# A decoder layer with fast-weight memory and routed experts: a new order of the router stage and other loads around it

## The chip, the cores and the metric

The kernel runs on one NeuronCore of one Trainium2 chip. The metric is the device time of one execution in microseconds (us). TensorE, VectorE (DVE), ScalarE (ACT), GpSimd (POOL) and SyncE (SP) each run their own instruction list in order and meet at semaphores; DMA transfers are issued by SyncE, ScalarE or GpSimd.

## What is computed

The layer takes x of 4 x 1024 x 512 and a context of 4 x 64 x 512, all in float32. It has three parts, each added onto x. Layer norm, softmax and top-k are the usual ones:

```python
x = x + attn(layernorm(x), W_qkv, W_out)          # 16 heads of 64, rotary, causal softmax
x = x + xattn(layernorm(x), ctx, ctx, Wq, Wk, Wv, Wo, bo, ...)
x = x + ffn(layernorm(x), router_w, router_b, we_gate, we_up, we_down)

# xattn: a memory M (32 x 32 per batch and head) is built from the 64 context rows
#   M = M - a * (M k) k^T + b * v k^T      row by row, k normalised
#   q = layernorm_per_head(query @ Wq.T) * gq + bq
#   out = (M q) @ Wo.T + bo
# ffn: top 2 of 8 experts per token, weights by softmax of the two logits
#   y = (silu(h @ we_gate[e]) * (h @ we_up[e])) @ we_down[e]
```

## The kernel before

Every matrix product that needs float32 accuracy is made of three products of a high and a low part (`parts`: high x high, high x low, low x high); the low part is the input less its high part. ScalarE writes high parts, VectorE or GpSimd low ones.

The program has four stages, each a room of buffers and semaphores with a barrier of all engines at its end. `context_phase` prepares context keys and values. `attention_phase` (512 units of one head and one row tile) does attention, and on GpSimd the recurrence of the memory; it leaves the unnormalised head outputs in `scr_attT` and the reciprocals of the softmax sums in `scr_rinv`. `memory_phase`, called the router stage here, goes over 32 tiles of 128 tokens: output projection of attention, residual, memory read-out, second residual, router logits, top 2, a position for each token in its experts' regions, and a scatter of the normalised rows into `scr_hs`. `expert_phase` runs 39 blocks of 256 rows, one expert each.

The router stage is a software pipeline written by hand. `sweep` runs `step(r, i)` on every engine: four steps unrolled, a loop of three rounds of eight steps, eight steps unrolled; so the loop has two back edges. At step i the tiles i, i-1, ... i-4 are at different points. TensorE does, in order: transposes of n2 of tile i-1 (`turn("n")`), the first half of the output projection of tile i into pA, transposes of qn (i-2), the second half, transposes of hn (i-3), the counting product pW (i-4), the query projection pQ (i-1), the memory product pM (i-2), the logits pR (i-3). A turn waits until the turn two before it has been read, so that the turn of hn waits for the low part of nT (`nlo`). At a batch change (i = 2, and then every eighth step) the memory of the next batch, laid out block-diagonally in `bd`, is multiplied by the output weights `wo` in four products of 512 columns into two banks in turn; VectorE must have taken the low part (`mwl`) of a bank's product before the bank is used again, and all four before pM.

VectorE's step in the kernel before: low parts of nT (L1614), qT (L1620) and of the attention rows ap (L1595); x2 = pA + x (L1629), its layer norm (L1601 to L1607), the low parts of a batch change (L1637); the per-head norm of the query (L1644 to L1658); x3 (L1665), its layer norm into hn, and the token column (L1673); logits and top 2 of tile i-3 (L1679 to L1694); positions of tile i-4 (L1702 to L1713). GpSimd adds the bias (x2b, L1398), makes qn = qc * hs3 (L1404), scales the attention rows of tile i+2 (L1389) and scatters tile i-4 (L1414).

Ahead of the first step the router stage loads 3 MB of weights into buffers that are free then, and splits them (L1297, L1522, L1587), behind which TensorE waits. After the last step, VectorE turns the expert counts into a table of blocks (L1721 to L1747), SyncE writes blocks of zeros behind each expert's rows (L1355), and after the barrier `expert_phase` fetches rows and the first weights.

## Time and profile before

| | us |
|---|---|
| median of 3 runs | 3069.8 |
| lowest, highest | 3062.35, 3074.35 |
| profiled execution | 3063.33 (span 3061.6) |
| context and attention, until TensorE stops | 0 to 1692.96 |
| router stage, TensorE's first to last product | 1728.41 to 2276.91 |
| expert stage, from its first product | 2318.96 to 3061.6 |

TensorE is busy for 2732.9 us (89% of the span), VectorE for 1981.9 (65%), ScalarE for 1666.9 (54%), GpSimd for 1481.4 (48%). These shares are means over stages with different limits; the rows further down look at one stage or one step each. In a row of the timeline the first number is the start, the second the duration, and brackets hold the idle time of the engine just before, with what ended it.

### The profile page before, as it was taken

To read this page: it belongs to the slowest core of one execution; us is meant where nothing else is said; L and a number is where in the kernel's file an instruction comes from. 1 tells how busy PE (TensorE), PEld (TensorE's weight loads), DVE (VectorE), ACT (ScalarE), POOL (GpSimd) and SP (SyncE) were. 2 spreads that over 40 slices of the span, in tenths; PEclk is the share of its full clock that TensorE was granted. 3 is DMA by queue.
4 is the path that set the end of the run, shared out by engine and by line. 5 is a ranking of instruction groups with operands and counts; after the bars stand their busy time and mean duration, and the time that the engine had idled before them with its cause. 6 is when DMAs were issued, how large, how long until landed. Compare 5 with 4: busy or idle time off the path is not lost. (4 is left out here: it accounts for less than half of the span.)

```text
span 3061.6 us, 49728 instructions
## 1 busy us (share of the span) xinstructions
PE 2732.9 (89%) x15887; PEld 2288.0 (75%) x15887; DVE 1981.9 (65%) x3907; ACT 1666.9 (54%) x3190; POOL 1481.4 (48%) x1606
## 2 busy tenths in 40 slices
PE   5899979999889999899998498889857999999998
PEld 3788868888778888688887377767645888888886
DVE  5477656677657676566667377778754666565555
ACT  2466655666656665566666233323315767776665
POOL 1567654766555666455564234434423334444443
PEclk8999999999999999999999699999978999999999
DMA  3644343435343434343433545455424444444433
GB/s 120 111 107 116 94 117 91 107 95 131 87 104 95 125 95 113 92 107 84 106 74 80 149 116 127 127 126 136 110 89 116 96 97 103 99 99 97 96 55 48
DMA packets 221099, 316.81 MB, mean 103 GB/s; under 512 B 60432, under 2 KB 139312, under 8 KB 217584
## 3 DMA queue, kind: packets, MB, share of 16 engines
q1 hardware_dynamic: 178256, 220.20, 29.6%
q0 software_dynamic: 42656, 94.31, 12.6%
q8 instruction: 94, 1.54, 0.2%
q14 instruction: 93, 0.76, 0.1%
HBM read 241.28 MB, written 75.17 MB: 103 GB/s over the span
## 5 line engine op out<-in xcount | busy, mean ns | idle before, releaser
L1010 ACT ACTIVATE a_pt<-a_PT 128x512 fp32r<-128x512 f32 (+3 forms) x768 | 350.4, 490 | 534.4 <-PE a_PT L876 533.6
L1084 DVE TENSOR_REDUCE a_nmax<-a_S 128x1 f32<-128x1024 f32 (+7 forms) x512 | 384.9, 752 | 266.7 <-PE a_S L865 265.5
L1093 DVE TENSOR_TENSOR a_pt<-a_PT,a_pt 128x512 fp32r<-128x512 f32 (+3 forms) x768 | 401.8, 550 | 190.6 <-ACT a_pt L1010 188.9
L893 PE MATMUL a_O<-a_pt,a_v 128*128 128x256 f32 (+1 forms) x2560 | 355.9, 286 | 49.5 <-DVE a_ot L1108 25.2
L999 ACT ACTIVATE a_pb<-a_S,a_nmax 128x1024 f32<-128x1024 f32 (+7 forms) x512 | 380.3, 743 | 17.8 <-DVE a_nmax L1084 17.8
L893 PEld LDWEIGHTS a_O<-a_pt,a_v 128*128 128x128 f32 x2560 | 325.9, 193 | 64.7 <-DVE a_ot L1108 30.8
L876 PE MATMUL a_PT<-a_ident,a_pb 128*128 128x128 f32 x2304 | 342.3, 276 | 35.3 <-DVE a_pt L1093 33.9
L1982 DVE TENSOR_TENSOR e_w<-e_raw,e_w 128x1024 fp32r<-128x1024 f32 x238 | 281.2, 1223 | 119.0 <-ACT e_w L1932 118.9
L876 PEld LDWEIGHTS a_PT<-a_ident,a_pb 128*128 128x128 f32 x2304 | 270.5, 141 | 78.5 <-issue 28.5
L863 PE MATMUL a_S<-a_kh,a_qs 128*128 128x512 f32 (+3 forms) x768 | 285.3, 372 | 1.7 <-DMA a_kl<-a_rot 1.7
L813 PE MATMUL a_Z<-early_xT,early_wq 128*128 128x512 f32 x512 | 239.2, 467 | 45.8 <-issue 16.9
L864 PE MATMUL a_S<-a_kl,a_qs 128*128 128x512 f32 (+3 forms) x768 | 258.4, 348 | 0.0
L739 POOL TENSOR_TENSOR a_rot<-a_tmp,a_rot 128x512 fp32r<-128x512 f32 x128 | 163.1, 1294 | 177.6 <-ACT a_rot L982 177.3
L1818 POOL DMA_INDIRECT out<-e_y,e_dest x78 | 140.3, 1798 | 201.4 <-ACT e_y L1941 187.8
L732 POOL TENSOR_TENSOR a_tmp<-a_tmp,a_part 128x512 f32<-128x512 f32 x64 | 82.4, 1287 | 311.8 <-DVE a_part L1059 311.8
L1932 ACT ACTIVATE e_w<-e_raw 128x2048 fp32r<-128x2048 f32 x119 | 227.8, 1914 | 6.6 <-DMA e_raw<-in_we,e_ix 6.2
L1814 POOL DMA_INDIRECT e_raw<-in_we,e_ix x122 | 153.1, 1255 | 153.4 <-issue 135.3
L815 PE MATMUL a_Z<-early_xT,early_wq 128*128 128x512 f32 x512 | 203.7, 398 | 0.0
L814 PE MATMUL a_Z<-early_xT,early_wq 128*128 128x512 f32 x512 | 203.1, 397 | 0.0
L813 PE MATMUL a_Z<-early_wv,early_xT 128*128 128x256 f32 x512 | 162.8, 318 | 2.0 <-DVE a_v L1076 2.0
L863 PEld LDWEIGHTS a_S<-a_kh,a_qs 128*128 128x128 f32 x768 | 147.1, 192 | 21.2 <-DMA a_kl<-a_rot 3.6
L864 PEld LDWEIGHTS a_S<-a_kl,a_qs 128*128 128x128 f32 x768 | 147.3, 192 | 17.3
(286 smaller groups left out, 7005.1 us busy)
## 6 DMA issues: line engine op xcount, KB each, us to landing
a_qs<-a_rot SPq DMA_DIRECT2D x256, 128.0 KB, 2.3
a_kh<-a_rot SPq DMA_DIRECT2D x256, 128.0 KB, 2.3
a_kl<-a_rot SPq DMA_DIRECT2D x256, 128.0 KB, 2.3
e_rows<-scr_hs SPq DMA_DIRECT2D x40, 516.0 KB
scr_attT<-a_ot SPq DMA_DIRECT2D x256, 64.0 KB, 2.1
m_att<-scr_attT SPq DMA_DIRECT2D x32, 512.0 KB, 4.4
m_rb<-scr_rinv SPq DMA_DIRECT2D x64, 256.0 KB, 9.0
a_raw<-in_wqk POOLq DMA_DIRECT2D x31, 512.0 KB, 4.2
```

What stands on the lines that cost most here:

```text
L813: pe.matmul(out, lhs(0), rhs(0), start=start, stop=False)
L815: return pe.matmul(out, lhs(1), rhs(0), start=False, stop=stop)
L863: pe.matmul(out, q, kh[:, sl, c0:c1], start=True, stop=False)
L864: pe.matmul(out, q, kl[:, sl, c0:c1], start=False, stop=c1 != cols)
L876: mm = pe.transpose(PT[(k + s) % 2][:, (kt % 4) * P:(kt % 4 + 1) * P], pb[u % 2][:, kt * P:(kt + 1) * P], ident[:, :])
L893: mm = pe.matmul(O[:, c0:2 * P], v2[:, n % 2, kt, h, :, :].rearrange("p a d -> p (a d)"), pt[j % 2][:, part, kt, c0:2 * P], start=kt == 0 ...
L999: act.activation(pb[u % 2][:, 0:cols], S[u % 2][:, 0:cols], ACT.Exp, bias=nmax[:, u % GU:u % GU + 1], scale=1.0, accum_out=rsum[:, b % 2, ...
L1010: act.activation(pt[u % 2][:, 0, 4 * s:4 * s + m, (qt % 2) * P:(qt % 2 + 1) * P], PT[(k + s) % 2][:, 0:m * P].rearrange("p (k q) -> p k q" ...
L1084: dve.tensor_reduce(nmax[:, u % GU:u % GU + 1], S[u % 2][:, 0:cols], AXX, ALU.max, negate=True).then_inc(s_nb, 1)
L1093: dve.tensor_tensor(pt[u % 2][:, 1, 4 * s:4 * s + m, q], PT[(k + s) % 2][:, 0:m * P].rearrange("p (k q) -> p k q", k=m), pt[u % 2][:, 0, 4 ...
L1932: act.activation(w[:, k, 0, :], raw[:, k, :], ACT.Copy).then_inc(s[f"whi{k}"], 1)
L1982: dve.tensor_tensor(w[:, k, 1, c], raw[:, k, c], w[:, k, 0, c].bitcast(F32), ALU.subtract).then_inc(s[f"wlo{k}"], 1)
```

## The change

**Seam ahead of the router stage.** The buffers `raw`, `cos`, `sin` and `tmp` of attention become parts of one buffer `stage`, which lives through all stages. In unit U-16 GpSimd loads the router stage's weights into it (`load_next`); the router stage splits them into the buffers that attention used for x and its weights. The loads of tile 0 stand ahead of the constants. `rinv` is stored so that a tile's rows are contiguous: one store for a batch, not four, and rows of 4 KB for the broadcast loads.

**Router stage.** The query weights are centred once per head (`centre`), so that the per-head mean of pQ is zero; the reduction, the mean and qc go. ScalarE squares pQ itself. qn is made by VectorE from pQ. The token, top and gap columns of hn go to GpSimd, hn has four slots instead of eight. VectorE's step has a new order, with the layer norm in two parts (`moments`, `norm`). A batch change's four products, high and low parts are spread over the step.

**Seam behind.** The fill positions are computed first; the table of blocks takes fewer, wider instructions. Four of the stores of zeros are issued by ScalarE, and that of the spare block stands ahead of the wait. The three weight matrices of expert 0 are loaded during the router stage, and the first fetch is skipped if the first block belongs to expert 0.

The core of the diff:

```diff
@@ attention_phase
+            def load_next():
+                last = NG * GH // 2 - 1
+                gp.wait_ge(s_zfree, zi[("q", last, 3)] + 1)
+                gp.wait_ge(s_rot, 4 * (last + 1))
+                gp.wait_ge(s_wlow, len(wcount))
+                for k in range(6):
+                    gp.dma_start(stage[:, k // 2, k % 2 * T:(k % 2 + 1) * T],
+                                 io["wmem"][k // 3][:, k % 3 * T:(k % 3 + 1) * T]).then_inc(s_wm, 16)
@@ memory_phase, sync
+            load_att(0, 0)
+            load_x(0, 0)
+            for dst, src in ((bo[:, :], io["bo"].partition_broadcast(P)),
+                             (wo[:, :, :], io["woT"].rearrange("(e p) n -> p e n", p=P))):
+                sp.dma_start(dst, src).then_inc(s["c"], 16)
+            load_att(0, 1)
+            load_x(0, 1)
...
+            sp.dma_start(dram["hs"][NE * REG:NE * REG + BLK, :].rearrange("(a p) d -> p a d", p=P),
+                         zero[:, :, :]).then_inc(s["zero"], 16)
             sp.wait_ge(s["fin"], 1)
-            for e in range(NE):
+            for e in range(NE // 2):
@@ memory_phase, gpsimd
-                    gp.tensor_tensor(qn[:, j % 2, :].rearrange("p (h j) -> p h j", h=XH),
...
+                    gp.tensor_scalar(hn[:, j % 4, C_TOK:C_TOK + 1], hn[:, j % 4, C_TOK:C_TOK + 1],
+                                     float(4 * P), None, ALU.add).then_inc(s["side"], 1)
+                    gp.tensor_tensor(hn[:, j % 4, C_GAP:C_GAP + 1], top8[:, j % QT, 0:1],
+                                     top8[:, j % QT, 1:2], ALU.subtract).then_inc(s["side"], 1)
+                    gp.tensor_copy(hn[:, j % 4, C_TOP:C_TOP + 1], idx[:, j % 2, 0:1]).then_inc(s["side"], 1)
...
+            gp.wait_ge(s["c"], 16 * 6)
+            gp.wait_ge(s["wl"], 6)
+            for k in range(3):
+                gp.dma_start(route["raw"][:, k, :], io["we"][0, k]).then_inc(s["pre"], 16)
@@ memory_phase, scalar
+                    act.wait_ge(s["Q"], t)
+                    act.activation(sq[:, :], pQ[:, :], ACT.Square).then_inc(s["sq"], 1)
...
+            for e in range(NE // 2, NE):
+                z = act.value_load(route["tab"][0:1, 3, e:e + 1], min_val=0, max_val=(NE - 1) * REG + TOK)
+                act.dma_start(dram["hs"][bass.ds(z, BLK), :].rearrange("(a p) d -> p a d", p=P),
+                              zero[:, :, :]).then_inc(s["zero"], 16)
@@ memory_phase, vector
+            def centre(k):
+                w = loaded(k).rearrange("p (h j) -> p h j", j=XD)
+                n = 3 * (k - 4)
+                mean = wmean[:, k - 4, :]
+                dve.tensor_reduce(mean, w, AXX, ALU.add).then_inc(s["wc"], 1)
+                dve.wait_ge(s["wc"], n + 1)
+                dve.tensor_scalar(mean, mean, 1.0 / XD, None, ALU.mult).then_inc(s["wc"], 1)
+                dve.wait_ge(s["wc"], n + 2)
+                dve.tensor_tensor(w, w, mean.unsqueeze(2).broadcast_to([P, 2 * XH, XD]),
+                                  ALU.subtract).then_inc(s["wc"], 1)
...
-                    dve.tensor_reduce(hs1[:, j % 2, :], q3, AXX, ALU.add).then_inc(s["hvar"], 1)
...
-                    dve.tensor_tensor(qc[:, j % 2, :].rearrange("p (h j) -> p h j", h=XH), q3,
...
+                    dve.tensor_tensor(qn[:, j % 2, :].rearrange("p (h j) -> p h j", h=XH),
+                                      pQ[:, :].rearrange("p (h j) -> p h j", h=XH),
+                                      hs3[:, j % 2, :].unsqueeze(2).broadcast_to([P, XH, XD]),
+                                      ALU.mult).then_inc(s["qn"], 1)
...
             ch.step(dve.tensor_copy(cnt[:, :], pW[:, 0:NE]))
+            ch.step(dve.tensor_tensor(fill[:, :], cnt[:, :], base[:, :], ALU.add))
+            dve.tensor_copy(route["tab"][:, 3, 0:NE], fill[:, :]).then_inc(s["fin"], 1)
@@ expert_phase, vector
-            ch.do(dve.memset(same[:, 0:1], 0.0))
+            ch.do(dve.tensor_scalar(same[:, 0:1], route["expert"][:, 0:1], 0.0, None, ALU.is_equal))
```

VectorE in a plain step of the router stage, from the add into x2 on. m_A0 is pA of tile i, m_Q the query projection, m_W the counts. Before:

```order
L1629 TENSOR_TENSOR m_x2<-m_A0,m_x 128x512
L1601 BN_STATS m_st<-m_x2 128x6
...
L1607 TENSOR_SCALAR m_n2<-m_x2,m_mv,m_rs 128x512
L1644 TENSOR_REDUCE m_hs1<-m_Q 128x16
L1645 ISA
L1648 TENSOR_SCALAR m_hs3<-m_hs1 128x16
L1651 TENSOR_TENSOR m_qc<-m_Q,m_hs3 128x512
L1655 TENSOR_REDUCE m_hs1<-m_sq 128x16
L1658 RECIPROCAL m_hs3<-m_hs2 128x16
L1665 TENSOR_TENSOR m_x3<-m_M,m_x2b 128x512
```

and now:

```order
L1718 TENSOR_TENSOR m_x2<-m_A0,m_x 128x512
L1677 BN_STATS m_st<-m_x2 128x6
...
L1679 BN_AGGR m_mv<-m_st 128x2
L1728 TENSOR_TENSOR m_pr<-m_W,m_base 128x8
L1729 TENSOR_TENSOR m_cum<-m_cum,m_msum 128x8
L1734 SCALAR_TENSOR_TENSOR m_junk,m_pf<-m_iota8,m_idx,m_pr 128x8 x2
L1739 CAST m_pi<-m_pf 128x2
L1684 RECIPROCAL m_rs<-m_sd 128x1
L1686 TENSOR_SCALAR m_n2<-m_x2,m_mv,m_rs 128x512
L1747 TENSOR_REDUCE m_hs1<-m_sq 128x16
L1755 TENSOR_TENSOR m_x3<-m_M,m_x2b 128x512
```

The counting of tile i-4 has moved from the end of the step to between the moments and the normalisation of x2, and three instructions on m_Q are gone from between n2 and the reduction of the squares.

TensorE at a batch change, where the products of bd and wo stand. Before:

```order
L1439 MATMUL m_A0<-m_ww,m_ap 128x512
L1470 ISA
L1477 MATMUL m_A1<-m_wo,m_bd 128x512
L1477 MATMUL m_M<-m_wo,m_bd 128x512
L1476 ISA
L1477 MATMUL m_A1<-m_wo,m_bd 128x512
L1476 REGISTER_ALU
L1477 MATMUL m_M<-m_wo,m_bd 128x512
L1448 MATMUL m_T0<-m_ident,m_hn 128x128 x4
```

and now, with the rows of the projections left out:

```order
L1501 MATMUL m_A1<-m_wo,m_bd 128x512
...
L1472 MATMUL m_A0<-early_xT,m_ap 128x512
L1501 MATMUL m_M<-m_wo,m_bd 128x512
L1481 MATMUL m_T1<-m_ident,m_qn 128x128 x4
...
L1501 MATMUL m_A1<-m_wo,m_bd 128x512
...
L1501 MATMUL m_M<-m_wo,m_bd 128x512
```

The four products stood behind the second half of the projection; now one stands behind the transposes of n2, one between the halves, one behind the second half and one behind the counting product.

## Rows read from the trace of the kernel before

**Rows 1.** Stretches: length, busy time (instructions) by engine, TensorE's clock, DMA share, GB/s.

```profile
1728.41:2276.91 548.50, 472.09 (x2273) 378.73 (x2273) 398.88 (x1136) 165.96 (x304) 216.23 (x156) 0.93 0.46 117
2276.91:2318.96 42.05, 2.18 (x8) 1.44 (x9) 14.77 (x58) 4.22 (x4) 6.69 (x10) 0.50 0.61 226
2318.96:3061.60 742.64, 728.46 (x3432) 589.84 (x3432) 440.71 (x665) 505.31 (x547) 301.27 (x237) 0.99 0.41 85
```

**Rows 2.** TensorE's waits in the router stage: total us, times, longest.

```profile
PE m_T L1448 <- DVE m_nT L1614: 42.0, 26, 4.8
...
PE m_A L1477 <- DVE m_mw L1637: 17.2, 4, 4.8
```

**Rows 3.** Timeline, TensorE, the turn of hn in a plain step.

```profile
2001.24 0.63 PE L1448 MATMUL m_T<-m_ident,m_hn 128*128 128x128 f32 x4 [1.48 <-DVE m_nT L1614]
```

**Rows 4.** Timeline, VectorE, one plain step, some of its rows.

```profile
1990.57 0.68 DVE L1644 TENSOR_REDUCE m_hs<-m_Q 128x16 f32<-128x512 f32 x1
...
1992.88 0.69 DVE L1655 TENSOR_REDUCE m_hs<-m_sq 128x16 f32<-128x512 f32 x1 [0.70 <-ACT m_sq L1567]
1993.95 0.25 DVE L1658 RECIPROCAL m_hs<-m_hs 128x16 f32<-128x16 f32 x1 [0.38 <-ACT m_hs L1569]
...
1996.17 0.16 DVE L1605 RECIPROCAL m_rs<-m_sd 128x1 f32<-128x1 f32 x1 [0.36 <-ACT m_sd L1573]
1996.37 1.68 DVE L1607 TENSOR_SCALAR m_hn<-m_x,m_mv,m_rs 128x512 f32<-128x512 f32 x1
...
1999.55 0.16 DVE L1702 TENSOR_TENSOR m_pr<-m_W,m_base 128x8 f32<-128x8 f32 x1
...
2000.41 0.69 DVE L1614 TENSOR_TENSOR m_nT<-m_T,m_nT 128x512 fp32r<-128x512 f32 x1
...
2005.06 0.55 DVE L1607 TENSOR_SCALAR m_n<-m_x,m_mv,m_rs 128x512 f32<-128x512 f32 x1
2005.52 0.69 DVE L1644 TENSOR_REDUCE m_hs<-m_Q 128x16 f32<-128x512 f32 x1
```

**Rows 5.** Timeline, GpSimd, the same step.

```profile
1995.37 2.40 POOL L1389 TENSOR_TENSOR m_att<-m_att,m_rb 128x1024 f32<-128x1024 f32 x1
...
2003.87 1.31 POOL L1398 TENSOR_TENSOR m_x2b<-m_x,m_bo 128x512 f32<-128x512 f32 x1
```

**Rows 6.** L1045 (ns min/median/max), and timeline of attention, GpSimd and VectorE.

```profile
L1045 DVE TENSOR_TENSOR early_xT<-a_raw,early_xT x12: 1224/1226/2183, 425.6 to 1254.9; 128x1024 fp32r<-128x1024 f32 x12
...
424.33 2.37 POOL L718 TENSOR_TENSOR early_wq<-a_raw,early_wq 128x1024 fp32r<-128x1024 f32 x1
...
425.60 2.18 DVE L1045 TENSOR_TENSOR early_xT<-a_raw,early_xT 128x1024 fp32r<-128x1024 f32 x1 [1.42 <-ACT early_xT L974]
```

**Rows 7.** Timeline, a batch change on TensorE, and VectorE at a back edge.

```profile
1874.05 0.63 PE L1448 MATMUL m_T<-m_ident,m_n 128*128 128x128 f32 x4
1880.48 1.02 PE L1477 MATMUL m_A<-m_wo,m_bd 128*128 128x512 f32 x2
...
1898.32 0.64 PE L1448 MATMUL m_T<-m_ident,m_n 128*128 128x128 f32 x4
...
1923.13 0.69 DVE L1614 TENSOR_TENSOR m_nT<-m_T,m_nT 128x512 fp32r<-128x512 f32 x1 [3.32 <-issue]
```

**Rows 8.** Timeline, the start of the router stage.

```profile
1723.25 2.34 POOL L1389 TENSOR_TENSOR m_att<-m_att,m_rb 128x1024 f32<-128x1024 f32 x1 [20.71 <-DMA m_rb<-scr_rinv]
...
1728.41 0.76 PE L1437 MATMUL m_A<-m_ww,m_ap 128*128 128x512 f32 x1 [36.44 <-DVE m_ap L1595]
```

**Rows 9.** Timeline of the seam behind; last row: DMA queue over 2289 to 2303, packets, MB.

```profile
2289.34 10.08 SPq L1355 DMA_DIRECT2D scr_hs<-m_zero  x8
...
2305.26 0.36 SPq L1793 DMA_DIRECT2D e_ident<-in_ident  x1
...
2318.96 0.79 PE L1858 MATMUL e_G<-e_w,e_hT 128*128 128x512 f32 x1 [5.05 <-DVE e_w L1982]
...
q1 hardware_dynamic: 2447, 4.76, 90.8%
```

More of the change, by code:

```diff
@@ L77, in program @@
             "wv": keep.enter_context(nc.sbuf_tensor("early_wv", [P, 2, ET, GH * HD], F32R)),
+            "stage": keep.enter_context(nc.sbuf_tensor("early_stage", [P, 3, ET * D], F32)),
         }
-        context_phase(nc, io, dram, scan, early)
-        attention_phase(nc, io, dram, scan, early)
-    with ExitStack() as keep:
+        with ExitStack() as first:
+            scan = {
+                "k2": first.enter_context(nc.sbuf_tensor("scan_k", [P, TC, XD], F32)),
+                "v2": first.enter_context(nc.sbuf_tensor("scan_v", [P, TC, XD // 2], F32)),
+                "ab": first.enter_context(nc.sbuf_tensor("scan_ab", [P, 2, TC], F32)),
+            }
+            context_phase(nc, io, dram, scan, early)
+            attention_phase(nc, io, dram, scan, early)
         route = {
@@ L84, in program @@
             "tab": keep.enter_context(nc.sbuf_tensor("tab", [P, 4, NTAB], I32)),
+            "raw": early["stage"],
         }
-        memory_phase(nc, io, dram, route)
+        memory_phase(nc, io, dram, route, early)
         expert_phase(nc, io, dram, route)
@@ L1203, in memory_phase @@
         tb = rm.sb("tb", [P, 4, NTAB])
+        fill = rm.sb("fill", [P, NE])
+        lower = rm.sb("lower", [P, NE, NE])
+        upto = rm.sb("upto", [P, NE, NE])
+        past = rm.sb("past", [P, NTAB, NE])
         pA = [rm.ps(f"A{i}", [P, 512]) for i in range(2)]
@@ L1220, in memory_phase, with weights, loaded, ww @@
             "st30 st31 "
-            "tot tb fin zero aux"
+            "tot tb fin zero side pre"
         ).split()
         s = {k: rm.sem(k) for k in names}
-        WPIECE = 2 * WCOLS // 3
-        hnf = hn[:, :, :].rearrange("p t d -> p (t d)")
-        wraw = [hnf[:, 0:WPIECE], hnf[:, WPIECE:2 * WPIECE], x2b[:, :, :].rearrange("p t d -> p (t d)")]
+        def weights(a, k):
+            return early["xT"][:, a, k, :] if k < ET else (
+                early["wq" if k == ET else "wv"][:, a, :, :].rearrange("p e n -> p (e n)"))
+        def loaded(k):
+            return early["stage"][:, k // 2, k % 2 * T:(k % 2 + 1) * T]
+        def ww(a, f):
+            half = slice(f % 2 * D, (f % 2 + 1) * D)
+            if f < 8:
+                return early["xT"][:, a, f // 2, half]
+            e = slice((f - 8) % 2 * 2, (f - 8) % 2 * 2 + 2)
+            return early["wq" if f < 10 else "wv"][:, a, e, :].rearrange("p e n -> p (e n)")
         CR = 2
@@ L1393, in step @@
                 t = r * QT + i
+                if here(r, i - 4) and after(r, i - 4, 2):
+                    gp.wait_ge(s[f"sc{(i - 6) % 4}"], 32 * (r * QT // 4 + (i - 6) // 4 + 1))
+                    gp.sem_inc(s["scd"], 1)
                 if here(r, i):
@@ L1463, in step @@
                     att_out(0, 4)
+                if b is not None:
+                    memory(1)
                 if here(r, i - 2):
@@ L1519, in _ @@
             act.sem_inc(s["ahi"], CR)
-            act.wait_ge(s["w"], 64)
-            for i in range(3):
-                act.activation(ww[:, 0, i * WPIECE:(i + 1) * WPIECE], wraw[i], ACT.Copy).then_inc(s["wh"], 1)
-            act.wait_ge(s["c"], 16 * 7)
-            act.wait_ge(s["pool"], 15)
+            for k in range(4):
+                act.activation(weights(0, k), loaded(k), ACT.Copy).then_inc(s["wh"], 1)
+            act.wait_ge(s["pool"], 17)
             def att_high(r, j):
@@ L1553, in step @@
                     act.activation(sd[:, 0:1], mv[:, 0, 1:2], ACT.Sqrt, bias=eps[:, 0:1]).then_inc(s["sd"], 1)
[L1554 to L1558 removed]
+                memory_high(2)
                 if here(r, i - 3):
@@ L1716, in _ @@
             att_low(0, 0)
+            for k in range(4, 6):
+                centre(k)
+            for k in range(4, 6):
+                weight_low(k)
             sweep(dve, step)
@@ L2009, in _ @@
             for t in range(RT):
+                weight_low(0, 0, t)
                 turn_low(0, t)
-            for k in range(2):
-                for h in range(2):
-                    weight_low(0, k, h)
+            for h in range(2):
+                weight_low(0, 1, h)
             with dve.Fori(0, NBLK) as j:
```

362 lines of the change are left out of this document (179 added, 183 removed).

## The prediction

> **What bounds the kernel now.** I read the stages first: the busy time of each engine in four stretches, cut where TensorE starts and stops [rows 1]. The router stage (1728.41 to 2276.91, 548.5 us) keeps TensorE busy for 472.1 us, so 76.4 us are lost there. The seam behind it (42.05 us) holds 2.2 us of TensorE work. The expert stage is 742.6 us with TensorE busy for 728.5: it is bound by TensorE and nothing in it moves. The third place is the seam ahead of the router stage, where TensorE waits 36.44 us [rows 8].
>
> Inside the router stage the list of TensorE's waits names the culprit: 42.0 us in 26 waits for VectorE's m_nT, 17.2 us in 4 waits for m_mw [rows 2]. In a plain step the transposes of hn wait 1.48 us for m_nT [rows 3]. VectorE's own order shows why [rows 4]: from one reduction of m_Q to the next (1990.57 to 2005.52) pass 14.95 us, and the only idle in it is waiting for small results of ScalarE (0.70, 0.38, and 0.36 ahead of each reciprocal L1605) and short gaps between instructions that need each other. VectorE sets the step; TensorE alone would need 14.95 - 1.48 = 13.47 us.
>
> **Router stage, VectorE's step.** From [rows 4], by starts:
> - Reduction of m_Q, mean, m_qc and the wait for the square: 1990.57 to 1992.88, 2.31 us, gone: the weights are centred instead, ScalarE squares m_Q itself, and L1655's counterpart starts at once.
> - The wait behind that reduction (0.38) is filled by the x3 work; both waits of 0.36 ahead of L1605 are filled by other work: -0.38 - 2 x 0.34 = -1.06.
> - The product qn comes from GpSimd to VectorE. It reads PSUM like L1614 (0.69 us): +0.69, and about +0.12 (an estimate, from the reciprocal's tail) because it needs the reciprocal just ahead.
> - The three side columns that go to GpSimd sat in or beside gaps of the top-2 chain, which stays as long as it is: 0.
> - The normalisation L1607 into m_hn takes 1.68 us where that into m_n takes 0.55 [rows 4]. GpSimd's product L1389 runs from 1995.37 to 1997.77 [rows 5], and m_hn ends 0.28 us behind it: it is held. In the new order m_hn comes at the end of a step, when GpSimd has no wide work: -1.13.
>
> 14.95 - 2.31 - 1.06 + 0.81 - 1.13 = 11.3 us of work. That would leave TensorE the bound at 13.47. But the holding moves. Call X the start of the add into x2. GpSimd adds x2b right after (1.31 us [rows 5], to about X + 2.05) and then, since qn no longer stands between, starts L1389 (2.40 us, to X + 4.45). VectorE's new order puts the counting of tile i-4 (0.86 us: 1999.55 to 2000.41 [rows 4]) and the normalisation n2 exactly there, from X + 1.8. A VectorE instruction with two SBUF inputs was held as well: L1045 took 2.18 us at 425.60, against a median of 1.23, while GpSimd's L718 ran to 426.70 [rows 6]. The counting has such instructions (m_cum, m_junk). If they are held to X + 4.5, n2 ends at about X + 5.9 where it could have ended at X + 3.3: +2.6, a step of 13.9. If only n2 is held (to X + 4.75) it costs 1.45, a step of 12.7, under TensorE's 13.47. Starts of wide instructions stand some 0.1 us closer than their durations, so I take 13.75, nearest to the held row; the ends are 13.47 and, if VectorE also meets ScalarE's chain late, 14.3.
>
> The Trainium skill (SBUF — State Buffer, section Who interferes with whom) says that a VectorE instruction with two SBUF inputs contends with a GpSimd instruction that reads SBUF, and that the later one blocks fully. It speaks against this order; by it the step is the 13.75 of the first case, without it 13.47. The trace shows it for one 1024-column instruction [rows 6] and for none of 8 columns.
>
> **Router stage, the sum.** Of the 31 intervals between transposes of n2, 20 are plain: 20 x 1.2 = 24 us. Three follow a batch change, where VectorE is less late already; I book 0.7 each: 2. A batch change took 1874.05 to 1898.32 = 24.3 us [rows 7], with one of the four waits for m_mw [rows 2]. Spread over the step, the four products add 3.4 us (1.02 each by the row, some 0.85 as their ends overlap). The last low part now comes behind n2 on VectorE: by the order above TensorE reaches the product with the memory about 3.3 us early. 13.5 + 3.4 + 3.3 = 20.2; the first one took about 22. I book 3.4 saved for each of four, 13 us; all hidden would be 7 each, nothing hidden 0. At the loop's two back edges VectorE stands 3.32 us with "issue" as releaser [rows 7], the longest of TensorE's waits for m_nT, 4.8 us, follows [rows 2], and a TensorE that has stood that long comes back at a lower clock (the stage's mean is 0.93 [rows 1]); VectorE has no slack to hide it, so I book only 2.8 each, 5.6. Start: centring two weight pieces (four passes over 1024 columns at 1.2 [rows 6], two low parts) stands ahead of the first x2 on VectorE, and one of them can be held by L1389: -2.5. The drain trades one late m_nT for an x3 add ahead of qn: 0. Sum: 42 us.
>
> **Seam ahead.** Before, 3 MB of weights and all constants were loaded and split first; rb of tile 0 landed so that L1389 started at 1723.25, and TensorE followed at 1728.41 [rows 8], 5.2 us later. Now the weights are loaded in the last 16 units of attention on GpSimd's queue, where the transfers have room, and ident, att and rb go first. The sums leave in one transfer, not four, which I book at 2 us (an estimate: three issues less): the stage starts near 1696.6. Four transfers issued by 1699.2, landed by 1704 to 1706 (rb now has rows of 4 KB; were it as slow as before, 9 us, 1708), then the same 5.2 us: TensorE at 1709.5, 19 us saved (15 to 21). The four pieces that the first products need (1.2 each on VectorE, [rows 6]) are split by 1703: hidden.
>
> **Seam behind.** VectorE's table chain and then nine stores of zeros stand in a row: counts at 2276.91, stores from 2289.34, ScalarE's and SyncE's next stage at 2305.26, first product at 2318.96 [rows 1, 9]. The fill positions now come first (stores from about 2278.6: -10.7), one store goes earlier (-1.4), the table chain (4.8 us) runs beside. But the nine stores moved 4.76 MB and filled the 16 DMA engines for 90.8% of 14 us [rows 9], 12.7 us: 8 of them take 11.3 us whichever engine issues them; and the last scatters (about 1 MB, 2 to 3 us) now fall among them. End 2295.1 against 2305.26: 10.2. Behind the barrier the first expert's weights lie ready, and the fetch skips: product after 11.4 instead of 13.7 us: 2.3. Together 12.5 us (8 to 17).
>
> The Trainium skill (DMA: Bandwidth & Descriptors, section Issuing engines are not separate DMA queues) says that spreading transfers over issuing engines saves only issue time. By that the split between SyncE and ScalarE is worth nothing here; if issue (1.26 us each, 10.08 for eight) had been the limit it would save 5 us more.
>
> **Sum.** 42 + 19 + 12.5 = 73.5 us from the profiled execution's 3063.3: 2990. The three runs lie between 3062.35 and 3074.35, median 3069.8; the profiled one is at their low end, so I say 2992.
>
> **Rivals.** (a) *Only the wide instructions are held*; TensorE bounds the step at 13.47 (+6), the products are hidden (+8), the rb rows land fast and the scatters don't disturb the stores (+6): 2972. For it: no row shows a small instruction held. Chance 0.22. (b) *VectorE stays the bound by more*: 14.3 a step (-11), batch changes and back edges give nothing (-15), the rear seam 8: 3023. For it: both places still have a long wait of TensorE's. Chance 0.17. (c) *Slower*: with its waits gone TensorE is granted less clock over the router stage. The stage's mean is 0.93 now [rows 1]. 13.47 us at full clock become 16.1 at 0.84, which eats the 73 us; below 0.83 the kernel is slower, at 0.8 by some 25 us, 3090. Against it: the expert stage runs at 98% busy with a clock of 0.99 [rows 1]. Chance 0.03. (d) *The seams don't do what they say*: the early loads in attention delay its last units, or the first fetch is not skipped, and the router gain alone stays, with a third of the seams (31.5 becomes 10.5): 3013. Nothing in the trace speaks for it. Chance 0.06. Forecast: 0.52.
>
> **Numbers.** The range reaches over (a) to (b): 2962 to 3026. A measurement of this kernel tells about 0.5% (15 us) from no change. All cases but (c) and a corner of (d) are beyond that: faster 0.95, same 0.02, slower 0.03.
>
> **What would show it.** TensorE's transposes of n2 should stand 13.5 to 13.8 us apart; L1607's counterpart for n2 near 2 us long, or one of m_cum and m_junk's far longer than 0.2, with GpSimd's product beside it; m_hn back at 0.55; the first product of the stage near 1709.5; the stores of zeros starting within 2 us of the counts and still filling the DMA engines for 11 us or more. I am wrong if the small instructions are never held and steps stay above 14, or if the clock of the router stage falls below 0.93.

## The result, and the profile after

The changed kernel takes **2991.4 us** (median of 4, 2985.8 to 2995.6) against 3069.3 us: a ratio of 0.9747, 95% interval 0.9721 to 0.9772. Its profiled execution took 2990.0 us, with a span of 2988.3; before it was 3061.6. All ratios are of fast runs: one run of c5_sp8 (3148.1 us at a granted clock of 0.83) and one of the kernel before beside c1 to c4 (4505.8 us at 0.56) were slow and are left out. The three stretches that answer to [rows 1] are these (same columns):

```profile
1715.30:2218.50 503.20, 465.85 (x2273) 378.53 (x2273) 404.04 (x983) 165.36 (x306) 200.96 (x222) 0.95 0.49 137
2218.50:2246.46 27.96, 2.18 (x9) 1.44 (x9) 8.77 (x28) 2.48 (x3) 6.54 (x12) 0.50 0.57 201
2246.46:2988.30 741.84, 726.55 (x3432) 589.73 (x3432) 441.11 (x666) 505.99 (x548) 320.75 (x236) 0.99 0.41 85
```

| stretch | before, us | after, us | saved | forecast |
|---|---|---|---|---|
| start to the last reciprocal of attention | 1692.5 | 1698.1 | -5.5 | 0 |
| from there to the first product of the router stage | 35.9 | 17.2 | 18.6 | 19 |
| router stage | 548.5 | 503.2 | 45.3 | 42 |
| seam behind | 42.05 | 27.96 | 14.1 | 12.5 |
| expert stage | 742.6 | 741.8 | 0.8 | 0 |
| sum | 3061.6 | 2988.3 | 73.3 | 73.5 |

The sum came out, but one row of the table was not foreseen (attention ends later), and inside the router stage some terms cancel. The forecast 2992 took 73.5 us from the profiled execution before, 3063.3, near the lowest of its runs (3062.35 to 3074.35); the medians are 77.9 us apart.

TensorE's waits from 1715 to 2220 (total us, times, longest), answering to [rows 2]:

```profile
PE m_M L1470 <- DVE m_mw L1695: 10.3, 4, 2.7
PE m_T L1481 <- DVE m_n L1686: 10.1, 2, 8.2
PE m_T L1481 <- DVE m_nT L1701: 6.6, 3, 2.2
```

The 26 waits for m_nT have become 3 (two at the back edges, one in the drain). A plain step of TensorE, VectorE and GpSimd (timelines, one step; the rows answer to [rows 4, 5]):

```profile
1817.83 0.63 PE L1481 MATMUL m_T<-m_ident,m_n 128*128 128x128 f32 x4
...
1831.27 0.63 PE L1481 MATMUL m_T<-m_ident,m_n 128*128 128x128 f32 x4
```

```profile
1811.92 0.68 DVE L1718 TENSOR_TENSOR m_x<-m_A,m_x 128x512 f32<-128x512 f32 x1
...
1813.63 0.45 DVE L1729 TENSOR_TENSOR m_cum<-m_cum,m_msum 128x8 bf16<-128x8 bf16 x1
1814.00 2.43 DVE L1734 SCALAR_TENSOR_TENSOR m_junk<-m_iota,m_idx,m_pr 128x8 f32<-128x8 f32 x1
...
1816.47 0.23 DVE L1734 SCALAR_TENSOR_TENSOR m_junk<-m_iota,m_idx,m_pr 128x8 f32<-128x8 f32 x1
...
1817.07 0.55 DVE L1686 TENSOR_SCALAR m_n<-m_x,m_mv,m_rs 128x512 f32<-128x512 f32 x1
...
1820.93 0.55 DVE L1686 TENSOR_SCALAR m_hn<-m_x,m_mv,m_rs 128x512 f32<-128x512 f32 x1
...
1825.37 0.68 DVE L1718 TENSOR_TENSOR m_x<-m_A,m_x 128x512 f32<-128x512 f32 x1
```

```profile
1812.77 1.28 POOL L1430 TENSOR_TENSOR m_x2b<-m_x,m_bo 128x512 f32<-128x512 f32 x1 [5.23 <-DVE m_x L1718]
1814.02 2.38 POOL L1418 TENSOR_TENSOR m_att<-m_att,m_rb 128x1024 f32<-128x1024 f32 x1
```

The transposes of n2 stand 13.44 us apart. Two m_junk instructions of the same shape, one behind the other, take 2.43 and 0.23 us: the first ends (1816.43) with GpSimd's product (1816.40). VectorE's step is 13.45 us too, with no gap over 0.15 us. So two things fit this trace: TensorE sets the step and VectorE just keeps up, or the other way round. The experiments begin there.

### The profile page after: what moved, and what is told of

Read it like the earlier page. It is cut to its first block and busy times, and to the rows that moved or that the text cites. A ratio compares the mean times of both kernels' runs of the same rounds, so it can differ in the third digit from the quotient of the medians.

```text
span 2988.3 us, 49627 instructions
## 1 busy us (share of the span) xinstructions
PE 2731.2 (91%) x15887; PEld 2292.6 (77%) x15887; DVE 1978.7 (66%) x3727; ACT 1663.8 (56%) x3193; POOL 1491.8 (50%) x1681
## 5 line engine op out<-in xcount | busy, mean ns | idle before, releaser
L2068 DVE TENSOR_TENSOR e_w<-early_stage,e_w 128x1024 fp32r<-128x1024 f32 x238 | 280.8, 1219 | 121.5 <-ACT e_w L2018 121.4
L741 POOL TENSOR_TENSOR a_rot<-early_stage,a_rot 128x512 fp32r<-128x512 f32 x128 | 162.9, 1291 | 178.3 <-ACT a_rot L997 178.0
L1904 POOL DMA_INDIRECT out<-e_y,e_dest x78 | 159.1, 2040 | 182.9 <-ACT e_y L2027 167.4
L2018 ACT ACTIVATE e_w<-early_stage 128x2048 fp32r<-128x2048 f32 x119 | 227.6, 1912 | 40.4 <-DMA early_stage<-in_we,e_ix 39.8
L734 POOL TENSOR_TENSOR early_stage<-early_stage,a_part 128x512 f32<-128x512 f32 x64 | 82.3, 1286 | 313.6 <-DVE a_part L1075 313.6
L1900 POOL DMA_INDIRECT early_stage<-in_we,e_ix x122 | 153.6, 1259 | 155.8 <-issue 137.2
L879 PEld LDWEIGHTS a_S<-a_kl,a_qs 128*128 128x128 f32 x768 | 147.7, 192 | 17.4
```

Source lines behind the costliest of these rows:

```text
L879: pe.matmul(out, q, kl[:, sl, c0:c1], start=False, stop=c1 != cols)
L2018: act.activation(w[:, k, 0, :], raw[:, k, :], ACT.Copy).then_inc(s[f"whi{k}"], 1)
L2068: dve.tensor_tensor(w[:, k, 1, c], raw[:, k, c], w[:, k, 0, c].bitcast(F32), ALU.subtract).then_inc(s[f"wlo{k}"], 1)
```

## Experiments

Eleven kernels ran, on three chips, each beside the kernel before: its median was 3068.7 us beside c1 to c4, 3068.5 beside c5 and c10 to c12, 3065.3 beside c6, c13 and c14. So the totals of two kernels of different groups are compared by their ratios, and where the intervals overlap (c2, c4, c5 and c6 with the changed kernel, c14 with c12) the totals show no difference; what these runs tell is read from their traces. All edits are to the changed kernel, if nothing else is said; "stage" is from the end of the first n2 to the counts (L1807), 487.5 us in the changed kernel.

| kernel | median, us | ratio to before (95%) | step | stage, us |
|---|---|---|---|---|
| changed | 2991.4 | 0.9747 (0.9721-0.9772) | 13.45 | 487.5 |
| c1_count_last | 3017.8 | 0.9835 (0.9809-0.9861) | 14.85 | 513.5 |
| c2_att_first | 2984.6 | 0.9722 (0.9704-0.9739) | 13.4-14.3 | 484.8 |
| c3_slack2 | 3019.4 | 0.9847 (0.9829-0.9865) | 14.75 | 515.9 |
| c10_side_first | 2978.8 | 0.9700 (0.9684-0.9716) | 13.45 | 477.5 |
| c11_side_slack2 | 2986.9 | 0.9721 (0.9703-0.9739) | 13.45 | 485.5 |
| c13_no_spread | 3001.7 | 0.9802 (0.9777-0.9828) | 13.45 | 501.8 |
| c4_late_load | 2982.7 | 0.9728 (0.9702-0.9753) | 13.45 | 487.8 |
| c5_sp8 | 2991.1 | 0.9743 (0.9724-0.9763) | 13.45 | 486.5 |
| c6_refetch | 2994.3 | 0.9771 (0.9751-0.9791) | 13.45 | 487.2 |
| c12_best | 2971.3 | 0.9683 (0.9666-0.9699) | 13.45 | 477.4 |
| c14_best2 | 2974.9 | 0.9703 (0.9682-0.9724) | 13.45 | 478.5 |

### The counting out of the way: c1_count_last

```diff
 # VectorE's step
-    counting of tile i-4     (between the moments of x2 and the normalisation n2)
     ...
     msum of tile i-3
+    counting of tile i-4
```

> The changed kernel with one edit: the counting of tile i-4 (five small VectorE instructions) stands at the end of VectorE's step and no longer beside GpSimd's product of the attention rows (L1418), so only n2 can still be held there. VectorE's work in a step falls from 13.45 us to about 12.3 (the first m_junk back from 2.43 to about 0.25, n2 held by up to 1.4 more). Theory T, TensorE sets the step (its own work is 13.47 us): transposes of n2 stay 13.46 us apart, VectorE gets about 1 us of idle time a step; the total moves only through the batch changes and back edges, -2 to -10 us, 2982 to 2990. Theory V, VectorE sets the step and the two agree by chance: TensorE's own step would have to be shorter than 13.46, the transposes come 12.5 to 13.2 us apart and the total falls by 8 to 30 us. Theory H, the small instruction was not held by GpSimd but is slow where it stands for another reason: m_junk stays near 2.4 us at its new place.

None of the three theories held: it became 26 us **slower**, and yet the small instructions were not held any more. VectorE and GpSimd in one step (timelines):

```profile
1813.79 0.23 DVE L1790 SCALAR_TENSOR_TENSOR m_junk<-m_iota,m_idx,m_pr 128x8 f32<-128x8 f32 x1
...
1819.11 3.95 DVE L1686 TENSOR_SCALAR m_n<-m_x,m_mv,m_rs 128x512 f32<-128x512 f32 x1
```

```profile
1816.04 1.79 POOL L1446 DMA_INDIRECT scr_hs<-m_hn,m_pi  x1 [0.83 <-POOL m_hn L1443]
1818.14 0.98 POOL L1446 DMA_INDIRECT scr_hs<-m_hn,m_pi  x1 [0.30 <-issue]
1819.13 1.31 POOL L1430 TENSOR_TENSOR m_x2b<-m_x,m_bo 128x512 f32<-128x512 f32 x1
1820.39 2.38 POOL L1418 TENSOR_TENSOR m_att<-m_att,m_rb 128x1024 f32<-128x1024 f32 x1
```

GpSimd waits for the counts (m_pi) before it scatters. Moved to the end of the step, the scatters fall where x2b stood, x2b starts 1.5 us later behind the add into x2 (1816.81), exactly when n2 is ready, and n2 is held through **both** of GpSimd's instructions: 3.95 us where 0.55 would do. What I overlooked: a moved step takes along everyone who waits for it. It shows that in this kernel the length of VectorE's step is a matter of who stands beside whom, and it leaves the question of the bound open.

### GpSimd's product elsewhere: c2_att_first

```diff
 # GpSimd's step
+    att_scale(r, i + 2)
     x2b = x2 + bo
-    att_scale(r, i + 2)
     side columns of tile i-4, scatters
```

> The changed kernel with one edit: GpSimd does its product of the attention rows (2.4 us) ahead of the add into x2b (1.3 us), not behind it. The hold should follow GpSimd's work. If an instruction with two SBUF inputs is held whatever its size: the first m_junk falls from 2.43 to at most 1.3 (it stands beside x2b only), and something at the end of VectorE's step, beside which the product now runs (m_hn, the low part of the attention rows L1672 of 1.2 us, or the reduction), becomes longer by 1 to 2.2 us. TensorE's step stays at 13.46 to 14, total 2988 to 3010. If the hold has to do with the place of the instruction and not with GpSimd: m_junk stays at 2.4.

The hold went with the product, as in the first case. Shapes of VectorE over the stage, sum in us and mean in ns; the first fence is the changed kernel, the second c2:

```profile
L1734 DVE SCALAR_TENSOR_TENSOR m_junk<-m_iota,m_idx,m_pr 128x8 f32<-128x8 f32 x62 | 64.8, 1046 | 1.1
...
L1686 DVE TENSOR_SCALAR m_hn<-m_x,m_mv,m_rs 128x512 f32<-128x512 f32 x32 | 17.5, 546 | 1.2
```

```profile
L1686 DVE TENSOR_SCALAR m_hn<-m_x,m_mv,m_rs 128x512 f32<-128x512 f32 x32 | 49.7, 1554 | 1.2
...
L1734 DVE SCALAR_TENSOR_TENSOR m_junk<-m_iota,m_idx,m_pr 128x8 f32<-128x8 f32 x62 | 13.8, 222 | 1.1
...
L1789 DVE CAST m_idx<-m_ix 128x8 f32<-128x8 uint32 x32 | 9.1, 283 | 3.4
```

m_junk fell from 64.8 to 13.8 us and m_hn rose from 17.5 to 49.7. Where the product came a little later, an 8-column cast was held instead (1.35 us at 1818.42, beside the product from 1817.19). Now VectorE's steps vary (13.25 to 14.4 us); TensorE waits 0.37 us for m_nT in a long one (14.01 us) and is back at 13.45 in the next, in which VectorE needs 13.25. That speaks for TensorE's own 13.45. The total came out below the 2988 to 3010 that I expected: the steps clear of batch changes cost 7 us more over the stage, but the start and the batch changes gave back 10.

### Who has slack: c3_slack2, c10_side_first, c11_side_slack2

```diff
 # c3: VectorE, end of each step (c11: the same on top of c10)
+    for k in range(2):
+        dve.bn_stats(extra[:, k, :], bo[:, :])
 # c10: GpSimd's step
     x2b = x2 + bo
-    att_scale(r, i + 2)
     wait for the counts, side columns of tile i-4
+    att_scale(r, i + 2)
     scatters of tile i-4
```

> The changed kernel with VectorE work added: two more statistics over a 512-column SBUF tensor (0.69 us each, 1.38 us together) at the end of each of its 32 steps, whose result nothing reads. VectorE's step of 13.45 us has no idle time in the trace. Theory T (TensorE sets the step and VectorE just keeps up): VectorE becomes the bound at about 14.8 us, 20 plain steps cost 1.3 us each and the rest some, total +30 to +45 us. Theory S (VectorE has hidden slack, its held instructions end with GpSimd's product anyway and later instructions fill the gap): less than half of it, +0 to +20 us.

> The changed kernel with one edit: GpSimd writes the three side columns of tile i-4 ahead of its product of the attention rows, the scatters behind it. So the product starts only behind VectorE's counting, about 4 us after the add into x2 (it was 2.1), when VectorE does a reduction, additions out of PSUM and statistics, which have stood beside GpSimd's work at their usual length so far. The first m_junk falls from 2.43 us to about 0.25, m_n stays at 0.55, VectorE's work in a step becomes about 11.1 to 11.6 us. Theory T (TensorE sets the step): transposes of n2 stay 13.45 us apart all the same, VectorE waits about 2 us a step, and only the four batch changes, the two back edges and the drain get shorter: -5 to -12 us. Theory V (VectorE sets it): steps of 11.6 to 13.2 us, -10 to -35 us. Theory M (the hold only moves to other instructions): VectorE's step stays at 13.4 and the total too.

> The kernel c10_side_first with the same added VectorE work as in c3_slack2 (two statistics of 0.69 us each per step, nothing reads them). In the changed kernel this work cost 28 us. If the hold of 2.2 us was what used up VectorE's slack, it now costs 0 to +8 us over c10_side_first and plain steps stay at 13.45. If VectorE is the bound for another reason, it costs about 28 us again.

In c3 a plain step grew from 13.45 to 14.75 us, nearly by the whole 1.38, and the total by 28, just under the 30 to 45 of theory T: VectorE had **no** slack. In c10 m_junk stands at its 0.22 us, the product runs beside a reduction and an addition out of PSUM that keep their length (the statistics begin only as it ends), and VectorE waits for TensorE. Timeline of c10, VectorE and GpSimd:

```profile
1815.99 0.22 DVE L1735 SCALAR_TENSOR_TENSOR m_junk<-m_iota,m_idx,m_pr 128x8 f32<-128x8 f32 x1
...
1817.31 0.68 DVE L1748 TENSOR_REDUCE m_hs<-m_sq 128x16 f32<-128x512 f32 x1
1819.20 0.69 DVE L1756 TENSOR_TENSOR m_x<-m_M,m_x2b 128x512 f32<-128x512 f32 x1 [1.22 <-PE m_M L1473]
1819.93 0.69 DVE L1678 BATCH_NORM_STATS2 m_st<-m_x 128x6 f32<-128x512 f32 x1
```

```profile
1817.53 2.37 POOL L1418 TENSOR_TENSOR m_att<-m_att,m_rb 128x1024 f32<-128x1024 f32 x1
```

Plain steps stayed at 13.45 all the same, and from 1790 to 1850, four plain steps, the list of TensorE's waits is empty, in c10 as in the changed kernel. So **TensorE bounds a plain step of the changed kernel at 13.45, and the hold of 2.2 us had used up exactly VectorE's slack** (theory T). Freed, the slack pays where VectorE is late, by the distances of TensorE's transposes: 0.9, 2.6 and 2.5 us in the last three batch changes and 2.5 in each of the steps with a back edge, nothing in the first batch change and nothing in the drain (0.7 lost there, 0.3 at the start). That makes 10.0 us in the stage; the medians differ by 12.6. And in c11 the 1.38 us a step cost 8 us instead of 28: 2.7 and 2.5 at the back edges, 2.4 behind the last transposes, nothing at the batch changes; plain steps stay at 13.4 to 13.5.

TensorE's waits there became shorter by 0.9 to 1.1 us each. Where the gain is larger than that, the granted clock rose with it. The first two rows are the second and third batch change of the changed kernel, the third its first back edge, the last the same back edge in c10:

```profile
1858.20:1877.99 19.79, 17.14 (x80) 12.64 (x80) 14.35 (x36) 7.07 (x14) 8.40 (x9) 1.00 0.44 135
1976.17:1997.57 21.40, 18.75 (x81) 13.80 (x80) 14.35 (x36) 7.07 (x14) 8.40 (x9) 0.92 0.50 133
1891.44:1908.83 17.39, 15.18 (x72) 12.34 (x72) 13.21 (x32) 5.25 (x10) 6.56 (x8) 0.90 0.50 130
...
1892.50:1907.42 14.92, 13.68 (x72) 11.14 (x72) 10.17 (x31) 4.83 (x9) 5.79 (x8) 1.00 0.48 138
```

Both batch changes hold one wait of 2.65 us, and the one at a granted clock of 0.92 takes 1.6 us longer. At the back edge the wait went from 2.21 to 1.24 us, the clock from 0.90 to 1.00 and the step from 17.4 to 14.9. Behind the wait of 2.21 us, products of 512 columns take 0.63 us for some 2 us (TensorE at the lower of its two clocks) and then 0.39 again.

### The memory's products in one piece: c13_no_spread

```diff
-    memory(0) ... memory(1) ... memory(2) ... memory(3)     (four places of the step)
+    for q in range(4): memory(q)                            (place of the fourth)
 # the same for ScalarE's high parts and VectorE's low parts
```

> The changed kernel with the memory's four products of a batch change, their high and their low parts each in one piece, at the place of the fourth (behind the ranks on TensorE, behind n2 on VectorE), instead of one at each of four places. If the spreading is what made a batch change 4.5 us shorter (24.3 to 19.8): now about 24 us each, total +15 to +20 us. If it was the shorter VectorE step that did it: 20 to 21.5 us each, total 0 to +7 us.

It cost 14.3 us in the stage (10.3 in the medians, 17 by the ratios), 2.2, 5.1, 3.4 and 3.5 us in the four batch changes, where I had expected 15 to 20 by the one theory and 0 to 7 by the other; it is the first theory's, a little smaller. The third product uses the bank of the first and stands in one wait until VectorE has done n2 and its low part:

```profile
1865.77 1.02 PE L1501 MATMUL m_M<-m_wo,m_bd 128*128 128x512 f32 x2
1871.62 2.08 PE L1501 MATMUL m_A<-m_wo,m_bd 128*128 128x512 f32 x2 [4.83 <-DVE m_mw L1689]
```

So 3.5 us for each of the four, on average, come from the spreading. Part of it is clock: the last three waits are 4.8 us at a granted clock of 0.86, in the changed kernel 2.65 us at 1.00, 0.92 and 0.92.

### The late end of attention: c4_late_load

```diff
-                if u == U - 16:
-                    load_next()
+            load_next()                 # behind the last unit, before the waits at the end
```

> The changed kernel with the early load of the weights taken out of attention: GpSimd issues the same six transfers behind its last attention unit. Attention ended 5.5 us later in the changed kernel (1697.7 against 1692.2). Theory L, the 3 MB under its last units delay it: attention ends at 1692 to 1694. Theory R, the delay comes from something else (the shared stage, the reordered sums, or chance): it stays at 1696 to 1698. Either way the router stage's first product comes later, at the earliest when 3 MB have landed (some 8 us at 390 GB/s) behind the ones of att and rb: total +3 to +15 us against the changed kernel's 2991.

Attention ended at 1693.1, and TensorE stood idle for 17.16 us from its last work of attention to the router stage's first product, in the changed kernel for 17.78: nothing was lost, because GpSimd is done with attention at 1670 and the transfers, issued at 1669.93, still land before the seam. I was wrong there (+3 to +15 expected, -8.7 measured in the medians, which their spread does not tell from 0). Is it the load, though? Here is the tail of attention, from the start of GpSimd's last pair of additions into a_rot to the start of the last reciprocal, in all traces, with the time that TensorE waited for a_kl's transfers behind 1600:

| load | tail, us | wait for a_kl, us | tail began at |
|---|---|---|---|
| none (before) | 56.0 | 0.2 | 1636.5 |
| early: changed, c1, c2, c3, c10, c11, c5, c6, c13 | 58.9, 57.9, 57.1, 61.7, 60.8, 57.3, 54.9, 57.1, 54.9 | 1.3, 1.2, 1.2, 2.7, 3.4, 2.0, 0.2, 2.8, 0.5 | 1635.4 to 1643.9 |
| late: c4, c12, c14 | 54.3, 54.3, 56.6 | 0.2, 0.2, 0.2 | 1636.6 to 1642.5 |

With the early load the tail is 2.8 us longer on average (57.8 against 55.1), though the ranges overlap. The waits tell more: seven of the nine waited over 1 us for a_kl's transfers, and none of the four others over 0.2. So the load under the last units costs something, about 3 us by these few traces. A stretch of 20 us between 1600 and 1680 at a granted clock of 0.74 to 0.94 stands in five of the early traces and in one of the late ones (c14, 0.93), 1.00 in the others; in the changed kernel it comes before the load is issued (1655.49), as in c1 and c11; only in c3 and c10 does it stand behind the load (0.74 and 0.76 from 1660 to 1680), and these two have the longest tails. Two stretches of the changed kernel:

```profile
1620.00:1640.00 20.00, 17.59 (x109) 14.97 (x109) 12.96 (x25) 12.81 (x33) 5.84 (x5) 0.94 0.06 15
...
1660.00:1680.00 20.00, 16.15 (x119) 13.80 (x117) 14.59 (x28) 14.38 (x36) 11.93 (x21) 1.00 0.69 202
```

(Before, the second stretch had a DMA share of 0.14 and not 0.69.) And the place where the tail begins moves by 8.5 us from trace to trace in the same code. Of the changed kernel's 5.5 us, 2.9 are the tail and 2.6 had passed before the load was issued: chance, as far as these traces tell.

### The seam behind: c5_sp8 and c6_refetch

```diff
 # c5: all stores of zeros by SyncE
-            for e in range(NE // 2):
+            for e in range(NE):
 # c6: the first fetch is not skipped
-            ch.do(dve.tensor_scalar(same[:, 0:1], route["expert"][:, 0:1], 0.0, None, ALU.is_equal))
+            ch.do(dve.memset(same[:, 0:1], 0.0))
```

> The changed kernel with all eight stores of zeros on SyncE, none on ScalarE. Theory B (the DMA engines limit them: 4.2 MB in about 11 us): the last store lands at the same time, the table chain (to 4.9 us behind the counts) is done anyway, and the seam stays at 28 us; total -1 to +2. Theory I (issue limits: 1.26 us a store, 10.1 us for eight): the last store is issued 5 us later, the barrier comes 3 to 5 us later, total +3 to +5.

> The changed kernel with the first expert's weights fetched again behind the barrier (the mark that lets the fetch skip them is set to 0); they are still loaded early as well. Prediction's theory: the ready weights are worth 2.3 us, measured in the traces 13.66 us (before) against 10.87 us (changed) from the barrier's end to the first product, so this kernel stands at 13 to 14 us there and the total is +2 to +4 us. Rival: the rows of tokens arrive last anyway (TensorE's wait in the seam is for e_rows), the seam stays at 28 us and the total within 1 us; then the 2.8 us came from the earlier ident and shorter queue instead.

The changed kernel, then c5, in rows of SyncE's and ScalarE's queues:

```profile
2220.03 5.22 ACTq L1639 DMA_DIRECT2D scr_hs<-m_zero  x4
...
2220.31 4.84 SPq L1384 DMA_DIRECT2D scr_hs<-m_zero  x4
...
2235.59 0.36 SPq L1879 DMA_DIRECT2D e_ident<-in_ident  x1
```

```profile
2211.72 11.45 SPq L1384 DMA_DIRECT2D scr_hs<-m_zero  x8
2227.10 0.36 SPq L1874 DMA_DIRECT2D e_ident<-in_ident  x1
```

Counts at 2218.54 and 2210.12: the barrier ends 17.05 and 16.98 us behind them, though the issues end at 6.7 and 13.05. Theory B: the split between two engines is worth nothing. In c6 the first product came 31.6 us behind the counts instead of 27.9: the early load of the first expert's weights is worth 3.7 us in this place (forecast 2.3). The medians differ by 2.9, the ratios by 7, with intervals that overlap, so the totals don't size it. The row shows what the longer seam waits for: ScalarE's conversion, for which a transfer that moves nothing is enough in the changed kernel (5.7 us behind the barrier's end), waits for the weights themselves (9.3 us):

```profile
2242.05 1.91 ACT L2018 ACTIVATE e_w<-early_stage 128x2048 fp32r<-128x2048 f32 x1 [31.78 <-DMA early_stage<-in_we,e_ix]
```

### Put together: c12_best and c14_best2

c12 is c10 and c4 together, and the rows of the second tile (att, rb, x) are loaded ahead of bo and wo. c14 moves the centring and splitting of the last weight piece from ahead of the first x2 to behind the first n2, and the early load of the first expert's weights one step later.

> The kernel c10_side_first, with the weights' early load issued behind GpSimd's last attention unit (as in c4_late_load) and the rows of the second tile loaded ahead of the bias and the memory's weights. Added up: -8 (c4 against the changed kernel), -5 to -12 (c10), and 2 to 5 us at the start of the stage, where the transposes of n2 came 15.8 us behind the first product because GpSimd waited 6.6 us for the second tile's rows and then held VectorE's split for 2.1: total 2968 to 2978. If the early load was not what ended attention late, or the reordered loads only make another load late, 2980 to 2988.

> The kernel c12_best with the second weight piece's centring and split (about 5.1 us of VectorE work) moved from ahead of the first tile's x2 to behind its n2, and the early load of the first expert's weights one step later. The add into the first x2 stood at 10.2 us behind the first product, TensorE's products of the tile end at 7.7: the first transposes of n2 should come 11 to 13 us behind the first product, not 15.4, and the total be 2 to 4 us below c12_best, 2967 to 2970. If GpSimd's x2b and product simply hold n2 longer then, nothing is gained: 2971 +- 2.

c12 is the best kernel here: 2971.3 us, 20 us below the changed one, the intervals of their ratios do not overlap. 12.6 of it is c10. c12 stands 7.5 below c10 on the same chip, its runs (2971.0 to 2975.3) all below c10's (2975.8 to 2981.1). In the two traces attention ends 9.4 us earlier in c12: 6.5 of it is a shorter tail, as the late load would have it, and 2.8 had passed before the tail. The reordered rows gave only 0.4 us at the start, because the hold moved: the mean's scaling (32 columns, 0.18 us otherwise) now takes 1.85 beside GpSimd's product. c14 gained nothing that can be told, as its rival had it: its first n2 ends 13.2 us behind the first product and not 15.3, but the second n2 is then held and TensorE waits for it:

```profile
1738.62 4.04 DVE L1690 TENSOR_SCALAR m_n<-m_x,m_mv,m_rs 128x512 f32<-128x512 f32 x1
```

## Why the prediction was right, point by point

**A plain step: the hold right, its size right to 0.3 us, the bound wrong by a hair.** The forecast had m_cum and m_junk held to X + 4.5 and n2 ending at X + 5.9; with X = 1811.92 the trace has 1816.43 and 1817.62, X + 4.5 and X + 5.7. m_hn went back to 0.55. Forecast 13.75, measured 13.45, 0.2 of the difference ahead of n2's end. Rival (a) said that small instructions are not held; they are. But its number, TensorE's 13.47, is the one that came out, since VectorE's work came out no longer than it. I had VectorE setting the step at 13.75; TensorE sets it at 13.45 (c10, c11). About 1.6 us were saved in each of the 15 steps that lie clear of batch changes, back edges and ends: 24.4 us. I had booked 24, with 20 steps of 1.2: too many steps and too little for each, and that the product agrees is luck.

The Trainium skill (SBUF — State Buffer, section Who interferes with whom) says that a VectorE instruction with two SBUF inputs, a copy, a cast or a tensor_scalar can contend with GpSimd and a reduction never does, and that the order of issue, not the shape, decides who blocks. The runs agree on the kinds and the shape: 8 columns were held 2.43 us, and in c10 the reduction of 512 columns took 0.68 beside the product. On the order the recorded starts are split. At the start of the changed kernel GpSimd's product, behind a two-input subtraction of VectorE that had started 0.09 us before it, took 3.40 us where 2.37 would do:

```profile
1719.28 3.40 POOL L1418 TENSOR_TENSOR m_att<-m_att,m_rb 128x1024 f32<-128x1024 f32 x1 [6.60 <-DMA m_rb<-scr_rinv]
```

But in c1 n2 has the earlier recorded start, by 0.02 us, and is the one that is held.

**Batch changes: right in the sum, 13.8 us for 13.** From transposes to transposes the four take 19.7, 19.8, 21.4 and 21.4 us (20.2 forecast) instead of 21.7, 24.3, 23.8 and 23.8. The 13.8 are taken by the ends of n2, with the step behind the first and the steps ahead of the others, which grew by 0.85: 2.3, 5.2, 3.2 and 3.1. So the second saved more than the 3.4 that I had booked, and the others less; the forecast had no clock in it. c13 shows that the spreading is the cause. **Back edges: too small.** 9.0 us in the two steps behind each, forecast 5.6, the term of the sum that was sized too low. VectorE's standstill for "issue" is still there (3.32 before [rows 7]), but TensorE waits 2.2 us for it where it waited 4.8, and the granted clock of the step went from 0.84 to 0.90. The prediction named this lower clock and gave it no price; c10, where the step runs at 1.00, shows that it has one.

```profile
1899.59 0.69 DVE L1701 TENSOR_TENSOR m_nT<-m_T,m_nT 128x512 fp32r<-128x512 f32 x1 [2.96 <-issue]
```

(The standstill in the changed kernel.)

**The start: the term that was sized worst.** The first n2 ends 15.8 us behind the first product and not 10.2, -5.6 where I had -2.5, and the next two steps lose 5.1 more, for which I had nothing. The passes that I listed come to 7.2 us (four of 1.2 and two low parts), and the prediction doesn't say why only 2.5 of them should count. In the trace the split of the wq piece is held (3.31 us), so that the add into x2 starts 10.7 us behind the first product and not 7.3, and then n2 itself (2.82, 0.55 before). **The drain: 0 forecast, 8.8 us measured** (the last two steps and the end behind the last n2, 37.5 instead of 41.6). VectorE's shorter chain shows there step by step; I read this from the traces and did not test it. 2.2 of the 8.8 come from where I cut: the last two steps have no product of GpSimd's, so n2 no longer ends late by the hold. Counted by the transposes the drain saves 6.6. Start and drain cancel (-8.2 and +8.8), and that the stage came out at 45.3 for 42 is in this part luck.

**Seam ahead: right, 18.6 for 19.** With attention's end at 1698.1 the stage's first transfer was issued at 1701.77; the product of the rows started at 1710.35 and TensorE 5.0 us later, by the same chain as before [rows 8]. The forecast time, 1709.5, missed only attention's lateness; c4's came at 1709.60. That lateness is in part a piece of rival (d), of which I had written "Nothing in the trace speaks for it"; the price was about 3 us, and the other 2.6 had passed before the load.

**Seam behind: right, 14.1 for 12.5.** Stores from 1.5 us behind the counts, the barrier at 17.05 (forecast 18.2), the first product 10.9 behind it (11.4). The DMA engines are full from the first store:

```profile
DMA  0004999999999997999999999989999999999999
...
q1 hardware_dynamic: 973, 1.91, 43.1%
q10 hardware_dynamic: 863, 1.68, 38.2%
q0 software_dynamic: 160, 0.53, 12.1%
```

(2220 to 2232, busy tenths of the 16 engines; then each queue's packets, MB and share; q0 holds the scatters.) The Trainium skill (DMA: Bandwidth & Descriptors, section Issuing engines are not separate DMA queues) says the same as c5: spreading saves issue time alone.

**Rival (c)** did not happen: the router stage's granted clock rose from 0.93 to 0.95.

**Not separated.** No run isolates what the seam ahead owes to the order of the loads, to the rows of 4 KB, to the single store and to the weights that are there already, nor what centring the weights gains in a step against what it costs at the start.

## What to carry to other kernels

Before moving a VectorE instruction, write down what GpSimd does beside it, and before moving a GpSimd instruction, what VectorE does: in this kernel a place beside reductions, statistics (0.69 us at 1812.64 beside x2b, as alone) and additions out of PSUM is free, and a two-input instruction, a cast or a normalisation stands until GpSimd's is done, however small it is. When two engines have the same step, add work to one and free work on it; only the pair of runs tells which sets the step and how much slack the other has. A wait of TensorE's costs more than its length where the granted clock falls with it, so the last microsecond of a wait can be worth two. A prefetch need not be issued as early as possible: in c4, c12 and c14 the load came 12 to 18 us later, TensorE's idle time in the seam stayed at 16.9 to 17.8 us, and a_kl's transfers did not wait.

## What the runs showed of the hardware that I had not expected

- A held VectorE instruction was not let in between two GpSimd instructions that follow each other: n2 took 3.92 to 4.00 us in most steps of c1, through x2b (1.3) and the product (2.4). The long m_junk of the changed kernel is the same case: it starts at 1814.00, while x2b still runs (to 1814.05), and the product goes first. In c14 n2 (4.04 us, from 1738.62) was held even beside three load issues of GpSimd (1738.32 to 1740.01) and then through the product.
- Size does not matter for the hold: 8 columns 2.43 us (0.23 free), an 8-column cast 1.35 (0.17), 32 columns 1.85 (0.18), 512 columns 2.49 (0.55).
- In nine executions with the same code in attention its end moves by 10 us (1690.9 to 1701.2), more than several of the effects looked for. By its total alone (2980.4 to 2992.6 against 2985.8 to 2995.6) c4's gain could not have been told from chance.
- In c1 the first scatter of a step took 1.72 to 1.97 us on GpSimd in most steps, 1.07 in the changed kernel, where it stands beside other VectorE work. Which of VectorE's instructions did that stays open.
- After the same wait of 2.65 us at a batch change the granted clock of the step was 1.00 once and 0.92 twice, in one execution of the changed kernel, and the step took 19.8 or 21.4 us. The waits of 1.7 us in c10 left it at 1.00 in the last three batch changes.
